# The edge-side mask of the fused attention stage, stored with the edge tile outermost

## The reference

```
h        = x W                                # per head
score(e) = leaky_relu(a_src.h[src e] + a_dst.h[dst e])
out[n]   = sum over edges e into n of  exp(score(e)) h[src e]  /  sum of exp(score(e))
```

## Time and profile before

| | |
|---|---|
| median of the runs | 6385.15 us (6381.38 to 6389.8) |
| profiled execution | 6378.63 us, span 6376.8 us |
| busy, of the span | TensorE 78%, weight loads 70%, VectorE 62%, ScalarE 28%, GpSimd 65% |
| granted TensorE clock, mean | 0.886 |
| fused stage | about from 430 us to 3300 us of the span |

### The profile page before, as it was taken

How to read it: one execution, slowest core, us unless ns; L and a number is a source line. 1 busy time by engine, 2 the same in 40 slices (tenths; PEclk the granted TensorE clock), 3 DMA queues, 4 the chain that set the end, 5 groups by cost and what they waited for, 6 DMA issues and landing times. The chain is left out here.

```text
span 6376.8 us, 102080 instructions
## 1 busy us (share of the span) xinstructions
PE 4984.9 (78%) x33831; PEld 4455.6 (70%) x33832; DVE 3977.4 (62%) x9818; ACT 1761.4 (28%) x4052; POOL 4158.7 (65%) x4039
## 2 busy tenths in 40 slices
PE   4427999999999999999985666666666666665887
PEld 3326999999999999999984545545555445545887
DVE  6526898888988898888963433343333333335676
ACT  2202444444444444444440000000000000003554
POOL 1347777777777777777727777777777777770111
PEclk9658999999999999999997777777777778777999
DMA  6555665556555665666624444444444444443211
GB/s 192 151 152 149 164 166 159 162 162 169 163 160 163 164 165 159 162 163 167 163 66 132 136 127 128 128 135 127 126 124 129 121 119 119 124 115 101 77 64 50
DMA packets 639158, 877.60 MB, mean 138 GB/s; under 512 B 254782, under 2 KB 447376, under 8 KB 638050
## 3 DMA queue, kind: packets, MB, share of 16 engines
q0 software_dynamic: 183392, 501.66, 27.5%
q1 hardware_dynamic: 424972, 334.16, 19.8%
q10 hardware_dynamic: 30326, 35.87, 1.7%
HBM read 766.70 MB, written 155.49 MB: 145 GB/s over the span
## 5 line engine op out<-in xcount | busy, mean ns | idle before, releaser
L1241 POOL DMA_INDIRECT m_ring<-tab_a,m_src x1764 | 1997.6, 1132 | 667.6 <-issue 504.7
L1859 POOL DMA_INDIRECT eb_rows<-tab_b,eb_src x1764 | 1713.6, 971 | 541.1 <-issue 537.0
L2100 PE MATMUL eb_acc<-eb_rows,eb_S 128*128 128x257 f32 x3528 | 1135.7, 493 | 497.7 <-DMA eb_rows<-tab_b,eb_src 496.4
L2100 PEld LDWEIGHTS eb_acc<-eb_rows,eb_S 128*128 128x128 f32 x3528 | 887.8, 257 | 707.1 <-DMA eb_rows<-tab_b,eb_src 521.9
L1522 PE MATMUL m_acc<-m_V,m_S 128*128 128x264 f32 x3528 | 862.4, 390 | 0.0
L1926 DVE TENSOR_TENSOR eb_sum<-eb_acc,eb_sum 128x257 f32<-128x257 f32 x98 | 41.8, 426 | 1228.3 <-PE eb_acc L2100 1228.3
L1522 PEld LDWEIGHTS m_acc<-m_V,m_S 128*128 128x128 f32 x3528 | 647.2, 192 | 93.5
L1643 ACT ACTIVATE mh_high<-m_ps,bn_b,bn_s 128x256 fp32r<-128x256 f32 x784 | 441.4, 563 | 750.6 <-PE m_ps L534 750.6
L522 DVE TENSOR_TENSOR mh_low<-mh_full,mh_high 128x512 fp32r<-128x512 f32 x784 | 544.1, 694 | 107.2 <-ACT mh_full L1643 76.4
L1632 ACT ACTIVATE mh_full<-m_ps,bn_b,bn_s 128x256 f32<-128x256 f32 x784 | 400.5, 563 | 669.3 <-DVE mh_low L522 346.1
L1316 DVE TENSOR_TENSOR m_V<-m_ring,m_V 128x1280 f32<-128x1280 f32 (+1 forms) x392 | 532.6, 1359 | 13.5
(11 more groups left out here) (372 smaller groups left out, 10321.4 us busy)
## 6 DMA issues: line engine op xcount, KB each, us to landing
m_dstb<-dst_p SPq DMA_DIRECT2D x196, 320.0 KB
m_dstb<-dst_p SPq DMA_DIRECT2D x196, 256.0 KB
buf<-empty SPq DMA_DIRECT2D x49, 771.0 KB
m_ring<-tab_a,m_src POOLq DMA_INDIRECT x1764
eb_rows<-tab_b,eb_src POOLq DMA_INDIRECT x1764, 2.8
xw_stage<-in_L_ffn_w_dram ACTq DMA_DIRECT2D x16, 1024.0 KB, 8.5
over<-b_blank SPq DMA_DIRECT2D x9, 1452.0 KB, 15.3
mOV<-over SPq DMA_DIRECT2D x49, 264.0 KB, 4.7
```

Of the source, the lines that this page charges most:

```text
L1241: gp.indirect_dma_start(out=ring[:, j, :], out_offset=None, in_=scratch["tab_a"], in_offset=bass.IndirectOffsetOnAxis(ap=src[:, j:j + 1], ...
L1859: gp.indirect_dma_start(out=rows_[q.par][j][:, t, 0:D], out_offset=None, in_=scratch["tab_b"], in_offset=bass.IndirectOffsetOnAxis(ap=src_ ...
L2100: last_i = nc.tensor.matmul(ps_acc[j][:, 0:NR], S[q.par][j][:, t, :], rows_[q.par][j][:, t, :], start=t == 0, stop=t == WT - 1)
```

## The change

The mask `ST` gets the edge tile as the outer dimension of its free part: [node, edge tiles, 128 edges]. The 128 columns of a weight are then neighbours. The build keeps its instruction and its input and writes through a rearranged view, edge by edge with the edge tile as the inner index, so that it still reads `dstb` in order.

```diff
-    ST = [sbuf(ctx, f"m_ST{i}", [P, P, QUARTERS[i]], BF16) for i in pair]
+    ST = [sbuf(ctx, f"m_ST{i}", [P, QUARTERS[i], P], BF16) for i in pair]
...
-                nc.vector.tensor_scalar(ST[s.side][:, :, :].rearrange("q p c -> q (p c)"), dstb[s.side][:, 0:s.size * P],
+                nc.vector.tensor_scalar(ST[s.side][:, :, :].rearrange("q c p -> q p c"),
+                                        dstb[s.side][:, 0:s.size * P].rearrange("q (p c) -> q p c", c=s.size),
                                         node_col[s.par][:, :], None, ALU.is_equal).then_inc(ST_ok, 1)
...
-                        last_i = nc.tensor.matmul(psE[s.side][:, j * 16:j * 16 + 2 * H], ST[s.side][:, :, j],
+                        last_i = nc.tensor.matmul(psE[s.side][:, j * 16:j * 16 + 2 * H], ST[s.side][:, j, :],
                                                   k["q3"][:, s.n, i, :], start=i == 2, stop=i == 0)
```

## The result

The changed kernel takes 6515.51 us (median of 6 runs, 6506.50 to 6518.36), the kernel before 6385.65 beside it: ratio 1.020, 95% interval 1.0188 to 1.0211. It is 130 us slower. The forecast was 6352 us; the range ended at 6412.

The account below looks back on a forecast made before the run. TensorE's instruction stream was taken as the bound: 1.20 us a group saved by dense weight loads, less 0.49 of stalls on VectorE, leaves 0.71, times 47 groups 33 us: 6352 us from a median of 6385.15, range 6326 to 6412.

Parts of the forecast that it names:

- What bounds the kernel before: Fused stage: TensorE's own instruction stream sets the pace, busy for all of 500 us, its largest wait 15.2 us in 2500.
- 25 ns a pair: TensorE's mask weight loads: dense pairs fall from 39 and 32.5 ns to 25, saving 1.20 us a group, 56 us.
- the rival with a floor of 32.5 ns for four-tile masks: TensorE's weight loads: four-tile masks gain nothing, 0.31 us a group is left, 15 us, 6370 us; chance 0.08.
- The hop at +0.83 ns a tick: VectorE's mask build: hopping writes add 0.27 us for a five-tile mask and 0.21 for a four-tile one.
- Its own sign for this, a build past 1.2 us: VectorE's mask build: passing 1.2 us would show the hop's price wrong and the run slower.
- The upper bound: VectorE's mask build: at worst the second element a tick is lost too, adding 0.86 and 0.69 us.
- slower rival: VectorE's mask build loses two elements a tick; TensorE loses 1.70 us against 1.20 gained, +24 us, 6409; chance 0.18.
- Both writes of a tick pay: VectorE's mask build: +1.66 ns a tick, 0.23 us a group left, 11 us, 6374 us; chance 0.12.
- Slack and stalls: TensorE's second-layer waits on VectorE's low halves: one delay of 0.49 us a group, at expert 4, leaving 0.71.
- The rival of free writes: VectorE's mask build: the hop costs nothing, the whole 56 us is kept, 6329 us; chance 0.18.
- The builds ahead of the loop: The 17 builds before the first body cost 0, since the loop waits there for gathered rows; at most 4 us.
- GpSimd's cover: GpSimd's gathers: waits of 3.4 us a group for staged indices cover the 2.6 that longer builds take.

Follow-up runs that it names:

- VectorE relieved: New layout with dense weights against the kernel before; the build writes only the mask's first half, in order, the rest stays zero: 6327.03 us, ratio 0.9916.
- the forms: Kernel before plus a phase of single VectorE comparisons, with nothing beside them: the changed build's form took 1649 ns, aligned pairs of bf16 555 ns.
- the forecast's own dose: Kernel with builds in runs of two, plus a maximum over 112 or 56 columns behind each build (257 and 201 ns): 6363.83 us, ratio 0.9964.
- runs of two: New layout and dense weights against the kernel before; the build writes two neighbouring bf16 elements, then hops 256 bytes: 6347.24 us, ratio 0.9944.
- experiment 4: Three dense-weight kernels against the kernel before: runs of two 6347.24 us, the even read hop 6435.73 us, a build of half the mask 6327.03 us.
- the even read hop: New layout against the kernel before; build writes in order, halves of the edges outermost, reading indices 20 or 16 bytes apart: 6435.73 us, ratio 1.0090.
- five-tile read hop: New layout, build writing in order tile by tile and reading five-tile indices 20 bytes apart; its kernel, against the one before: 6420.12 us, ratio 1.0057.

## Why the prediction was wrong

- **What bounds the kernel before: right.** TensorE's stream set the pace; with VectorE relieved, the group shortens by 57.05 - 55.92 = 1.13 us, nearly all that the weight loads gain, while the waits that TensorE had before stay as they were.
- **25 ns a pair: right.** It holds with 16 columns moving too; the rival with a floor of 32.5 ns for four-tile masks is refuted by the run of 0.29 us.
- **The hop at +0.83 ns a tick: the step that failed.** It measured (1649 - 554) / 320 = +3.42 ns a tick, four times as much. The rows it came from read and write 4-byte elements; for those it holds at steps of 16 bytes and more (+0.7 to +1.05). None wrote 2-byte elements with a step; the prediction says so, and took the 4-byte price all the same. Its own sign for this, a build past 1.2 us, is what came. The upper bound failed with it: +0.86 and +0.69 us had been put as the worst, +1.135 and +0.917 came. It had been built from one possible loss, that of the second element a tick, at the same price of a hop.
- **The slower rival had the right sign by a wrong mechanism.** Two elements a tick are kept, as far as the forms tell; what is lost is dearer. "Both writes of a tick pay" is wrong in kind too: a tick with one hopping write costs 4.44 ns and one with two 4.47, so the price goes by the tick and not by the write.
- **Slack and stalls: right in place, short in extent.** The waits of the second layer stand where they were forecast, at experts 3 and 4, but at expert 7 and at the accumulation as well: 3.4 us a group. With the forecast's own dose the chain gave 0.47 us a group instead of 0.71, and 6362 on the time of before instead of 6352. The stall for the dose was priced too high (0.49 us, measured 0.2 to 0.3), and some 0.5 us a group goes even with builds as short as before, which the forecast did not have. The rival of free writes, 6329 with the whole gain kept, fails on this too: runs of two are that case and gave 6347. (That their 34 us are near the forecast's 33 is chance.) The chain had been followed as far as expert 5 only, and without the third layer. The larger error by far is the price.
- **The builds ahead of the loop, "0, at most 4 us": wrong.** The loop starts 14.6 us later. Ahead of the first body TensorE waited 79.4 us for masks in 16 places instead of 66.7 in 12, 12.7 us more; with 17 builds of about 1 us more, not 0.24, VectorE is late there itself. The waits from 430 to 570 us, before and after:

```profile
PEld m_psE L1509 <- DVE m_ST L1286: 66.7, 12, 12.3
```

```profile
PEld m_psE L1510 <- DVE m_ST L1286: 79.4, 16, 12.4
```

- **GpSimd's cover: held here.** Its wait stayed at 132.7 us, though gathers grew from 1132 to 1189 ns. The cover was reckoned from staging alone; experiment 4 shows that a build of the forecast's length can use it up.

## What to carry to other kernels

Take the price of a strided access from a row with the same element size on the same side: on VectorE a 2-byte write with a step of 16 bytes cost over four times a 4-byte one, and where no such row exists the upper bound is not the sum of the losses one can name. When a layout must be turned, write it in runs that fill 4 bytes: here the same turn cost 555 ns instead of 1649, and it made this change 34 us faster instead of 130 slower. When a gain on the bounding engine puts a load onto the next, count that engine's idle time a group and follow its chain of waits to the group's end, not only to the first late instruction: here 0.5 us of the 1.2 a group went even without a longer build.

## What the runs showed of the hardware

- bf16 writes of VectorE: two a tick 256 bytes apart cost 4.47 ns a tick against 1.04 in order; 10 bytes apart, five tiles wide, 1983 ns for 640 elements; runs of two aligned elements 555 ns, runs of four or eight 802 and 790 ns. The last two write full words and read longer rows of single elements 20 bytes apart; the even read hop, which reads so too, took as long (789 ns). That points at the reads, without a run that shows it.
- The five-tile read hop loses two a tick (1348 ns), the four-tile one keeps it (673 ns), and with two halves outermost five tiles keep it as well (789 ns). The Trainium skill's VectorE: DVE Perf Modes (Mode 2×_2P) asks for an outermost dimension that is even on both sides or equal; the five of the read side meets a written side that is one run of 640, which agrees.
- A gather of 947 ns on GpSimd took 1149 to 1432 beside some forms of VectorE and 947 beside others, whether these went one or two elements a tick.
